# A routed feed-forward layer: the down weights of all eight experts stay in SBUF, and TensorE picks them by a register

## The reference, cut to what matters

```
gates = softmax(x @ Wg)                       # 8 experts
top_g, top_i = top_k(gates, 2)                # two experts for each row
top_g = top_g / top_g.sum()
y_e = (silu(x @ W1[e]) * (x @ W3[e])) @ W2[e] # W1, W3: 128x256, W2: 256x128
out = sum over the row's two experts of top_g * y_e
```

## Time and profile before

| | |
|---|---|
| runs | 1049.53, 1042.6, 1041.3 us; median 1042.6 us |
| the profiled execution | 1041.37 us; from the first to the last instruction 1039.5 us |
| TensorE busy | 880.4 us (85%) |
| VectorE busy | 716.8 us (69%) |
| granted TensorE clock, mean | 0.909 of 2.4 GHz |
| the last layer's 46 tiles on TensorE | 924 to 1010 us |

### The profile page before, as it was taken

The page is one execution under the profiler, slowest core; times in us unless marked ns, Lnnn a source line. Parts: engine busy times, 40 slices in busy tenths (PEclk is TensorE's granted clock), DMA queues, the critical chain, the costliest instruction groups (busy, mean ns, idle before and its releaser), DMA issues.

```text
span 1039.5 us, 18009 instructions
## 1 busy us (share of the span) xinstructions
PE 880.4 (85%) x5990; PEld 437.0 (42%) x5997; DVE 716.8 (69%) x1526; ACT 553.9 (53%) x653; POOL 409.5 (39%) x765
## 2 busy tenths in 40 slices
PE   6699999999999877599965988999999978879870
PEld 4223233232222444379952433333333323269860
DVE  6779999999999768634436596787678745453245
ACT  3488898889889522222224403545554554635440
POOL 4154552452453510078881502333333332434325
PEclk8599999999999999799986568999999998989885
DMA  5831011001110311147744423113211120439953
GB/s 174 264 109 47 15 33 46 26 20 45 52 34 1 100 54 45 32 108 186 181 62 134 162 93 94 48 47 95 94 47 46 47 68 1 150 85 328 306 187 81
DMA packets 72846, 97.31 MB, mean 94 GB/s; under 512 B 9752, under 2 KB 52600, under 8 KB 69304
## 3 DMA queue, kind: packets, MB, share of 16 engines
q1 hardware_dynamic: 64240, 86.29, 26.6%
q0 software_dynamic: 7680, 8.66, 4.2%
q10 hardware_dynamic: 864, 1.57, 0.4%
HBM read 75.46 MB, written 24.18 MB: 96 GB/s over the span
## 4 chain that ended last, share of the span: by engine, by line
PE 53%; DVE 24%; issue 9%; DMA 5%; POOL 4%; ACT 3%; SPq 2%; DVEq 0%; POOLq 0%; ACTq 0%
PE acc_ps L874 10%; PE acc_ps L1216 7%; DVE mx L574 6%; PE tail_ps L1162 6%; DVE R L1757 4%; PE causal_ps L1199 4%; PE causal_ps L1373 3%; DVE tails L1763 3%; PE causal_ps L836 3%; POOL moe_rows L2483 2%; PE causal_ps L847 2%; DMA ring<-e_pack 2%; PE causal_ps L1072 2%; PE tail_ps L1072 1%; ACT EX L1615 1%
## 5 line engine op out<-in xcount | busy, mean ns | idle before, releaser
L1615 ACT ACTIVATE EX<-causal_ps 128x1024 f32<-128x1024 f32 (+1 forms) x160 | 147.1, 938 | 156.8 <-PE causal_ps L1199 155.9
L574 DVE TENSOR_REDUCE mx<-tail_ps 128x1 f32<-128x512 f32 x266 | 157.5, 633 | 39.6 <-PE tail_ps L1165 21.6
L1465 ACT ACTIVATE R<-R 128x2048 f32<-128x2048 f32 (+1 forms) x80 | 134.7, 1737 | 0.5 <-DVE R L1757 0.5
L1199 PE MATMUL causal_ps<-QE,KE 75*128 75x512 bf16 (+3 forms) x384 | 103.1, 339 | 8.2 <-DVE mx L574 3.1
L1162 PE MATMUL tail_ps<-KM,QM 72*128 72x512 bf16 (+1 forms) x320 | 102.5, 347 | 8.8 <-DVE mx L574 3.0
L2538 POOL TENSOR_TENSOR pacer<-eps_ln 128x1 f32<-128x1 f32 x140 | 27.1, 194 | 201.2 <-ACT EX L1615 200.5
L1757 DVE TENSOR_SCALAR R<-causal_ps 128x1024 f32<-128x1024 f32 (+1 forms) x88 | 93.9, 1069 | 15.2 <-PE causal_ps L836 14.0
L1472 ACT ACTIVATE R<-R 128x1792 f32<-128x1792 f32 (+4 forms) x80 | 100.5, 1268 | 0.0
L1763 DVE TENSOR_REDUCE tails<-causal_ps 128x1 f32<-128x768 f32 (+4 forms) x96 | 92.8, 967 | 10.6 <-PE causal_ps L847 9.9
L2397 POOL TENSOR_TENSOR R<-R 128x512 f32<-128x512 f32 (+2 forms) x64 | 87.3, 1379 | 1.3
L1216 PE MATMUL acc_ps<-EX,VS 128*32 128x512 f32 (+3 forms) x768 | 85.1, 518 | 1.5 <-DVE EX L2228 1.5
(11 more groups left out here) (361 smaller groups left out, 1663.6 us busy)
## 6 DMA issues: line engine op xcount, KB each, us to landing
ring<-e_pack SPq DMA_DIRECT2D x46, 384.0 KB
QS<-q_parts SPq DMA_DIRECT2D x8, 576.0 KB
KS<-k_parts SPq DMA_DIRECT2D x24, 192.0 KB
QM<-q_parts SPq DMA_DIRECT2D x8, 576.0 KB
KM<-k_parts SPq DMA_DIRECT2D x24, 192.0 KB
QE<-q_parts SPq DMA_DIRECT2D x8, 576.0 KB
KE<-k_parts SPq DMA_DIRECT2D x24, 192.0 KB
wg<-in_wg_t SPq DMA_DIRECT2D x16, 256.0 KB
```

Of the source, the lines that this page charges most:

```text
L574: return reduce(mx[:, par, hh, o0:o0 + step * (cnt - 1) + 1:step], scores[:, 0:cnt * w].rearrange("p (c w) -> p c w", w=w), AX.X, op, **how)
L1199: mm = pe.matmul(causal_ps[hh % 2][:, c0:c1], KE[0:MROWS, par, hh, kt * P:(kt + 1) * P], QE[0:MROWS, par, hh, q0:q0 + c1 - c0], start=True ...
L1465: act.activation(R4[:, rp, h0:h0 + 2, 0:width], R1[:, rp, h0:h0 + 2, 0:width], ACT.Square).then_inc(squared, 1)
L1615: act.activation(EX[:, rp, hh, 0:width], causal_ps[hh % 2][:, 0:width], ACT.Exp, scale=float(D) ** -0.5).then_inc(exp_done, 1)
```

## The change: what it does

- `e_pack` and `ring` hold the two up weights alone. A tile's DMA brings 256 KB instead of 384 KB. The number of these DMAs and their place in SP's list stay.
- A new tensor `w_down_all` in SBUF holds the down weights of all eight experts, 1 MB, loaded by one DMA at the start of the program, where two DMAs had copied them to `e_pack`. The SBUF taken is the same: `ring` gives 8 KB in each partition, `w_down_all` takes it.
- TensorE reads the tile's expert from `owner` into a register (`value_load`, in `down`) for each of the 46 tiles, and forms the address of the down weight from it.
- `blank`, the zeros that are written to `sent_rows` at the start, is half as long, since both halves are now filled from the same zeros.

```diff
-EW = 3 * F1
+EW = 2 * F1
...
         ring = sb("ring", [P, 2 * RING, EW], F32)
-        blank = ring[:, :, :].rearrange("p s w -> p (s w)")[:, 0:B * TILES * P].rearrange("p (b t w) -> p b t w", b=B, w=P)
+        w_down_all = sb("w_down_all", [P, E1, F1 // P, P], F32)
+        blank = ring[:, :, :].rearrange("p s w -> p (s w)")[:, 0:TILES * P].rearrange("p (t w) -> p t w", w=P)
...
-            for m in range(F1 // P):
-                sp.dma_start(e_pack[:, :, 2 * F1 + m * P:2 * F1 + (m + 1) * P], a["w2"][:, m * P:(m + 1) * P, :]
-                             ).then_inc(packed, 16)
+            sp.dma_start(w_down_all[:, :, :, :], a["w2"].rearrange("e (m p) d -> p e m d", p=P)).then_inc(packed, 16)
...
                 elif u == 0:
                     pe.wait_ge(ln_x, 2 * CH + CH)
-                w = ring[:, 2 * ((b * PAIRS + t // 2) % RING) + t % 2, :]
+                if t == 0:
+                    pe.wait_ge(f_owner, b + 1)
+                e = pe.value_load(owner[0:1, b, t:t + 1], min_val=0, max_val=E1 - 1)
                 for m in range(F1 // P):
                     mm = pe.matmul(banks[6 + u % 2][:, 0:P], hid_f[:, u % 3, m * P:(m + 1) * P],
-                                   w[:, 2 * F1 + m * P:2 * F1 + (m + 1) * P], start=(m == 0), stop=(m == F1 // P - 1))
+                                   w_down_all[:, bass.ds(e, 1), m, :].rearrange("p o d -> p (o d)"),
+                                   start=(m == 0), stop=(m == F1 // P - 1))
                 mm.then_inc(f_y, 1)
...
-            pool.memset(blank[:, :, :, :], 0.0).then_inc(zeros_set, 1)
+            pool.memset(blank[:, :, :], 0.0).then_inc(zeros_set, 1)
```

More of the change, by code:

```diff
@@ L629, in _ @@
                 sp.dma_start(sent_rows[b].rearrange("(t p) w -> p t w", p=P),
-                             blank[:, b, :, :]).then_inc(packed, 16)
+                             blank[:, :, :]).then_inc(packed, 16)
             for at, name in ((0, "w1"), (F1, "w3")):
                 sp.dma_start(e_pack[:, :, at:at + F1], a[name]).then_inc(packed, 16)
-            for m in range(F1 // P):
-                sp.dma_start(e_pack[:, :, 2 * F1 + m * P:2 * F1 + (m + 1) * P], a["w2"][:, m * P:(m + 1) * P, :]
-                             ).then_inc(packed, 16)
+            sp.dma_start(w_down_all[:, :, :, :], a["w2"].rearrange("e (m p) d -> p e m d", p=P)).then_inc(packed, 16)
             for j in range(NQ // 2 - 1):
@@ L735, in _ @@
                          ).then_inc(f_gate_in, 16)
-            sp.wait_ge(packed, 16 * (B + 2 + F1 // P))
+            sp.wait_ge(packed, 16 * (B + 3))
             def load_pair(b, q):
@@ L2570, in fetch @@
                                             ).then_inc(arrived, 16)
-            pool.wait_ge(packed, 16 * (B + 2 + F1 // P))
+            pool.wait_ge(packed, 16 * (B + 3))
             for b in range(B):
```

## The result

The changed kernel took 1046.35 us (median of 20 runs, 1042.63 to 1055.83), the kernel before 1043.17 us in the same comparison. The ratio is 1.0039 with a 95% interval from 1.0021 to 1.0058: slower by 2 to 6 us, a loss, though within the 1% that the text ahead calls no change. Measured again later beside other kernels the ratio was 1.0059 (1.0032 to 1.0086). The forecast was 1046 us, so the total came out. Not all of its terms did, and that the two agree to 0.4 us is chance: the sum said +5.0 us, the medians rose by 3.2 us here and by 6 us in the later comparison.

The account below looks back on a forecast made before the run. TensorE's work (2.68 us per two tiles) barely exceeds a latency loop (2.55), which the pick makes longest. First half +5.3 us, given back between the halves, second half +5.0: 1046 us, forecast 1044 to 1051, 8 in 10 from 1038 to 1058.

Parts of the forecast that it names:

- The mechanism: In `down`, the register load waits for the product, so its whole length delays `down`; slack there is only 0.19 us.
- p: Delay from a tile's product on DVE to its `down`, taken as 0.85 us; about 23 us of time per us.
- the dear pick: Rival: every tile's register load between product and `down` as long as SP's longest, delay 1.12 us, 1053 us; chance 0.16.
- First half: Up to the last `down` of the half: +0.80 first `down`, +4.95 for 22 tiles, -0.42 stall gone; sum +5.3 us.
- Between the halves: Weights and TensorE arrive together at about 969 us; idle 3.36 us and clock fall go, first half's loss given back entirely.
- The rival in which the stall stays: Between the halves, `got` and SP's order hold weights back; 3.36 and 2.0 us return, 1051 to 1052 us; chance 0.07.
- Second half: Tile 25 to the last result: +3.15 for pace, +1.60 at DVE's two stops, +0.31 for the last `down`; sum +5.0 us.
- the last term: Last two `down` behind DVE's second stop: second register load follows the first, 0.80 us apart instead of 0.49, +0.31 us.
- Loads: 46 x 128 KB less to load, 5.9 MB; worth nothing apart from the two stalls, as TensorE waits for no other load.
- the empty array: Rival: each register load waits until TensorE's array is empty, four tiles take 10.3 us, 1088 us in all; chance 0.06.
- the falling clock inside a half: Rival: gaps of 0.2 to 0.8 us in every tile drop TensorE to 1.2 GHz, +14 us, 1060 us; chance 0.04.
- The hidden pick: Rival: register load runs ahead of the product, only stalls count; 1036 us, about 1041 if `got` still delays; chance 0.07.

Follow-up runs that it names:

- after, again: The changed kernel, unchanged, profiled and measured a second time beside other kernels; ratio to the kernel before 1.0059 (1.0032 to 1.0086).
- the changed kernel with the new order: Changed kernel, with SP loading the second half's first weights between its first 4 tiles and the other 19; ratios to the kernel before 1.0078 and 1.0057.
- the kernel before with the new order: Kernel before, with SP loading the second half's first weights between its first 4 tiles and the other 19; ratio 0.9989 (0.9962 to 1.0016).
- the smaller transfers alone: Changed kernel without its register load: tile t takes expert t modulo 8's down weight, leaving out the choice of expert; 1040.11 us, ratio 0.9960 to the kernel before.
- the early pick: Changed kernel with the register load moved from `down` to the end of `up`, ahead of the wait; 1041.49 us, ratios to the kernel before 0.9967 and 0.9991.

## Why the prediction was right, term by term

**The mechanism** held: the pick is bare between product and `down`, and 0.2 us of slack do not cover it. The register load's price was bounded by SP's rows and came out at the lower end wherever the load had its common length: p = 0.78 to 0.79 against 0.85, with bounds of 0.78 and 1.07. The Trainium skill, "DMA: Bandwidth & Descriptors", section "Latency and other measured facts", gives about 600 ns as the floor of a `tensor_load`; the 301 ns on TensorE disagree with it as SP's 274 did, and the dear pick that would have made it 1053 us did not come.

**The terms**, as difference to before, in us:

| stretch | predicted | after | after, again |
|---|---|---|---|
| first `up` to `down` 22 | +5.3 | +7.3 | +6.1 |
| `down` 22 to `up` 25 | -5.3 | -2.8 | -4.1 |
| `up` 25 to `up` 39 | +3.15 | +2.4 | +3.1 |
| `up` 39 to the last copy | +1.9 | +1.0 | +1.0 |
| sum | +5.0 | +7.9 | +6.0 |

*First half.* With p = 0.79 the prediction's own sum would be 0.74 + 5.5 x 0.78 - 0.42 = +4.6. What it missed: some register loads are long. In each of the two profiles about 1.5 us in all lie over 0.30 us in the first half's 23 loads, up to 0.85 us for a single one, each bare. The first profile adds a slower start: clock 0.63 in the 12 us behind the first `up`, where before and the repeat have 0.76.

*Between the halves: the step that failed.* The prediction let weights and TensorE arrive together, at about 969 and 969.4 us, and gave all of the loss back. SP's timeline, at the place of the earlier trace rows, and behind it the chain of waits:

```profile
958.88 1.41 SPq L755 DMA_DIRECT2D got<-sent_rows  x2
961.86 4.04 SPq L746 DMA_DIRECT2D ring<-e_pack  x2
```

```profile
965.54 5.87 DMA ring<-e_pack
971.42 0.04 issue
971.46 3.46 PE causal_ps L1372 x16
```

The weights landed at 965.54 + 5.87 = 971.41. Counted from the first `up` of the phase that is 5.5 us later than before, and 3.5 us in the repeat, where the prediction had 1.6. SP came to the tiles 4.0 us later (958.88 - 924.66 against 956.37 - 926.18; 3.0 in the repeat), not some 2. And the smaller loads gave nothing back: from there to the landing it took 12.5 us (11.5 in the repeat) against 11.1 before. The repeat's rows for the same:

```profile
959.83 1.41 SPq L755 DMA_DIRECT2D got<-sent_rows  x2
```

```profile
966.82 4.52 DMA ring<-e_pack
```

In the repeat TensorE came just in time for this:

```profile
970.00 0.60 PE L1359 MATMUL causal_ps<-ident,got 128*128 128x128 f32 x4
971.39 2.05 PE L1372 MATMUL causal_ps<-got_t,ring 128*128 128x128 f32 x16 [0.79 <-DMA ring<-e_pack]
...
975.18 1.06 PE L1372 MATMUL causal_ps<-got_t,ring 128*128 128x128 f32 x8
```

And in the first profile 0.7 us too early (its idle time begins at 971.46 - 1.55 = 969.91, that of the repeat at 970.60):

```profile
971.46 3.46 PE L1372 MATMUL causal_ps<-got_t,ring 128*128 128x128 f32 x16 [1.55 <-DMA ring<-e_pack]
```

"Together" was right for the repeat, if 2 us later than forecast, and there the clock stayed at 1.00: the 16 matmuls took 2.05 us. In the first profile the clock fell behind the 1.55 us of idle time. Its clock in the stretch behind them, then that of the repeat:

```profile
971.40:973.60 2.20, 2.14 (x10) 2.14 (x11) 0.00 (x0) 0.03 (x1) 0.00 (x0) 0.50 0.60 154
```

```profile
971.30:973.50 2.20, 2.11 (x19) 2.11 (x20) 0.42 (x1) 0.41 (x2) 0.00 (x0) 1.00 0.76 253
```

At 0.50, which is 1.2 GHz, 10 matmuls ran in the time of 19. So 0.7 us of arrival lie between 3.46 and 2.05 us for the two `up`. Even in the repeat tile 25 comes 2.0 us later than the sum has it. The longer first half is 0.8 of that. ACT's copy of the transposed tiles, which the sum left out and which TensorE sees bare once it no longer waits for weights, is 0.73. The other 0.44, from 975.18 - 971.39 = 3.79 in place of 3.35 us, is in the main a long register load again, that of tile 23 with 0.73 us:

```profile
L1385 PEldq TENSOR_LOAD <-owner x1: 729/729/729, 973.5 to 973.5; - x1
```

The four transposes behind the two `up` cost nothing, as the prediction had it: in the changed kernel with the new order tile 23's load had the common length, and with the same transposes it is 973.18 - 969.84 = 3.34 us to the `up` of tile 25.

```profile
969.84 2.02 PE L1376 MATMUL causal_ps<-got_t,ring 128*128 128x128 f32 x16 [0.73 <-issue]
971.70 0.60 PE L1363 MATMUL causal_ps<-ident,got 128*128 128x128 f32 x4
...
973.18 1.06 PE L1376 MATMUL causal_ps<-got_t,ring 128*128 128x128 f32 x8
```

The rival in which the stall stays had named this place and a late SP; its 5.4 us are two to four times what was missing from the give-back (2.5 and 1.2 us).

*Second half.* Right in pace: from tile 25 to 39 four tiles took 6.65 and 6.85 us, forecast 6.70. The difference to before is smaller than forecast since the kernel before took 5.97 us here, not 5.80. The end of the phase cost less than forecast by luck: the pick at DVE's stops did cost, but the clock held. Behind the first stop, the weight loads of `up` and `down` of the kernel before, and then of the changed one:

```profile
1000.15 1.72 PEld L1373 LDWEIGHTS causal_ps<-got_t,ring 128*128 128x128 f32 x8
1001.76 0.97 PEld L1386 LDWEIGHTS acc_ps<-ring,hid_f 128*128 128x128 f32 x4
1002.61 1.49 PEld L1373 LDWEIGHTS causal_ps<-got_t,ring 128*128 128x128 f32 x8
```

```profile
1006.17 0.97 PEld L1372 LDWEIGHTS causal_ps<-got_t,ring 128*128 128x128 f32 x8
1007.07 0.53 PEld L1387 LDWEIGHTS acc_ps<-w_down_all,hid_f 128*128 128x128 f32 x4
1007.51 0.97 PEld L1372 LDWEIGHTS causal_ps<-got_t,ring 128*128 128x128 f32 x8
```

Before, (1.72 - 0.97) + (0.97 - 0.53) + (1.49 - 0.97) = 1.7 us were lost at the low clock, which the prediction did not see in its rows; after, none. That is not the change's doing. Behind the same stop the clock is at 0.61 in the kernel before and at 1.00 in the kernel before with the new order; the changed kernel with the new order has 0.62 there in one profile. Where the clock holds, it is 15.3 us from `up` 39 to the last copy without the pick (the kernel before with the new order) and 17.9 with it, so the picks cost some 2.5 us where the sum has 1.9. Most of the excess lies in the last term, the second of two picks in a row: the last two results lie 1.59 us apart (1.15 in the repeat) in place of 0.44.

*Loads* were worth more than nothing, if little: the smaller transfers alone gave 1 to 7 us by the interval; the early pick, which has them too, 3.4 and 0.9 us by its two ratios. In the second half they took small waits that the prediction put at nothing: from tile 25 to 39 four tiles took 5.73 us with the smaller transfers alone and 5.97 before.

*The rivals*: the empty array and the falling clock inside a half did not come (6.5 to 7.6 us for four tiles, clock 1.00 from 936 to 962). The hidden pick was put at 1041 us where `got` still sets the second half's start; it did not come either, but the early pick, which hides the pick by its place, took 1041.5 and 1040.7 us.

So the mechanism and its price were right, and the total was right through errors of both signs, which is luck: the common p was 0.06 too high (worth 1.4 us), while long loads and an incomplete give-back cost 3 to 4 us more than the sum had, and the end of the phase 1 us less by a clock that held.

## What to carry to other kernels

A register load for an address costs by its place in the list, not by itself: behind the wait for the data it is bare in every tile, a tile earlier it is free. Where two limits lie close together (here 2.68 us of work, 2.55 us of latency for two tiles), relieving the third (the transfers) brought little, and any delay on the loop comes through almost in full (18 to 21 us of time for each us of delay, where 23 would be all of it). A stall that "goes away" in a forecast needs both arrival times, and all that stands between them and the work (here ACT's copy); here 0.7 us lay between a profile in which the clock fell and one in which it held.

## What the runs showed of the hardware

- A register load that TensorE's list issues ahead of need runs beside its matmuls: 46 loads of 306 ns median left the pace at 1.34 us.
- Such loads are sometimes long, on TensorE up to 0.85 us against 0.30 (8 and 7 of 46 over 0.4 us in the two profiles of the changed kernel), on SP up to 0.79 us in the same profiles. What makes them long no run shows.
- Two executions that run the same program ahead of the tile phase reach it 6.5 us apart, with granted clocks of 1.00 and 0.91 from 700 to 780 us. Behind the same stop of DVE the clock fell in some profiles and not in others, of kernels with and without the pick. A difference of a few us between two single profiles of this kernel says nothing of an edit.
